# Attention and feed-forward on one core: two batches' head-sum transposes and the last batch's key and query transposes in other units

## The reference, cut to what matters

```python
x = hidden
x = x + global_latent_attn(rmsnorm(x, norm1_w), g_wq, g_kv_down, g_k_up, g_v_up, g_wo)
x = x + local_gqa_attn(rmsnorm(x, norm2_w), l_wq, l_wk, l_wv, l_wo)
...
q, k = (rope(q, BASE_L), rope(k, BASE_L))
q, k = (qk_norm(q), qk_norm(k))
scores = jnp.einsum('bhqd,bhkd->bhqk', q, k) / np.sqrt(HD).astype(np.float32)
probs = jax.nn.softmax(scores, axis=-1)
return jnp.einsum('bhqk,bhkd->bhqd', probs, v)
```

## Time and profile before

| what | us |
|---|---|
| median of 3 runs | 1248.83 |
| lowest and highest of them | 1248.32, 1250.73 |
| the profiled execution's time | 1250.4 |
| its span, first to last instruction | 1248.6 |
| the attention stream in it, first exponential of unit 144 to the last addition to the state | 390.5 to 508.2 |

### The profile page before, as it was taken

One profiled execution on the slowest core, in us unless ns is written; L12 is line 12 of the kernel. 1 busy time (PEld: TensorE's weight loads), 2 busy tenths in 40 slices (PEclk: granted clock), 3 DMA queues, 4 the chain that ended last, 5 costly groups with the idle time before them and its releaser, 6 DMA issues.

```text
span 1248.6 us, 37433 instructions
## 1 busy us (share of the span) xinstructions
PE 1122.8 (90%) x16018; PEld 693.9 (56%) x16018; DVE 969.4 (78%) x1540; ACT 815.5 (65%) x1197; POOL 382.5 (31%) x536
## 2 busy tenths in 40 slices
PE   4488889898889989688999999999999999999985
PEld 3133434344445766455666666666666666666662
DVE  6969694869768688886887788778877887887755
ACT  3498898989878857355655665666566555656641
POOL 1203220201201014665533333343334333433310
PEclk8599999999999989898999999999999999999997
DMA  3113131022113541110211111111111100101102
GB/s 108 34 23 129 47 107 34 19 93 95 34 50 119 169 151 54 51 27 19 75 28 23 28 28 23 28 28 23 28 23 28 27 22 21 34 22 23 28 6 68
DMA packets 41684, 61.71 MB, mean 49 GB/s; under 512 B 7440, under 2 KB 16816, under 8 KB 41520
## 3 DMA queue, kind: packets, MB, share of 16 engines
q1 hardware_dynamic: 39728, 58.44, 16.0%
q10 hardware_dynamic: 1792, 0.87, 0.3%
HBM read 22.61 MB, written 16.78 MB: 32 GB/s over the span
## 4 chain that ended last, share of the span: by engine, by line
PE 52%; DVE 4%; ACT 2%; issue 1%; DVEq 0%; ACTq 0%
PE psum L1374 9%; PE psum L1510 7%; PE psum L1463 6%; PE psum L1485 5%; PE psum L1449 5%; PE psum L1384 4%; PE psum L1394 4%; PE psum L1536 3%; PE psum L1471 2%; PE psum L1434 2%; PE psum L1406 2%; ACT ffn_probs L1693 2%; PE psum L1440 1%; PE psum L1414 1%; PE psum L1502 1%
## 5 line engine op out<-in xcount | busy, mean ns | idle before, releaser
L863 ACT ACTIVATE att_probs<-psum 128x1024 f32<-128x1024 f32 x352 | 335.2, 1027 | 39.0 <-PE psum L721 38.8
L1804 POOL TENSOR_TENSOR ffn_rot<-ffn_rot,ffn_rot_sin 128x512 f32<-128x512 f32 x128 | 160.0, 1271 | 373.4 <-DVE ffn_rot L1835 373.4
L762 PE MATMUL psum<-att_probs,att_v 128*32 128x256 f32 (+3 forms) x3072 | 178.1, 346 | 3.8 <-DVE att_probs L1056 3.2
L721 PE MATMUL psum<-att_q_stack,att_k_parts 64*128 64x512 bf16 (+2 forms) x1472 | 134.4, 276 | 42.0 <-ACT att_probs L863 30.8
L721 PEld LDWEIGHTS psum<-att_q_stack,att_k_parts 64*128 64x128 bf16 x1472 | 45.6, 95 | 141.5 <-ACT att_probs L863 103.6
L1686 ACT ACTIVATE ffn_max_t<-psum 68x128 bf16<-68x128 bf16 x64 | 17.5, 273 | 156.8 <-PE psum L1422 156.6
L762 PEld LDWEIGHTS psum<-att_probs,att_v 128*32 128x32 f32 x3072 | 79.5, 110 | 63.5 <-issue 38.9
L1056 DVE TENSOR_TENSOR att_probs<-att_probs,att_causal_mask 128x1024 f32<-128x1024 f32 (+1 forms) x80 | 94.8, 1201 | 25.7 <-ACT att_probs L863 25.4
L1693 ACT ACTIVATE ffn_probs<-psum 128x1024 f32<-128x1024 f32 x64 | 65.6, 1025 | 59.2 <-PE psum L1449 59.2
L1655 ACT ACTIVATE ffn_sq<-psum 128x512 f32<-128x512 f32 x128 | 74.6, 595 | 21.8 <-PE psum L1374 20.9
L1463 PEld LDWEIGHTS psum<-ffn_v_back,ffn_probs 128*64 128x64 f32 x1024 | 64.5, 137 | 31.8 <-ACT ffn_probs L1693 18.0
(11 more groups left out here) (225 smaller groups left out, 2404.0 us busy)
## 6 DMA issues: line engine op xcount, KB each, us to landing
ffn_v_back<-ffn_v SPq DMA_DIRECT2D x120, 130.0 KB, 2.4
att_q_stack<-q_rows SPq DMA_DIRECT2D x28, 512.0 KB, 3.7
q_rows<-att_q_high SPq DMA_DIRECT2D x21, 256.0 KB, 2.8
q_rows<-att_q_mid SPq DMA_DIRECT2D x21, 256.0 KB, 2.6
q_rows<-att_q_low SPq DMA_DIRECT2D x14, 256.0 KB, 3.6
xres<-in_hidden SPq DMA_DIRECT2D x4, 512.0 KB, 6.2
out<-ffn_qk_t SPq DMA_DIRECT2D x3, 512.0 KB, 3.2
tail_f_wqkv<-in_f_wqkv SPq DMA_DIRECT2D x1, 768.0 KB, 5.5
```

What stands on the lines that cost most here:

```text
L721: ins = T.matmul(psum[:, banks[i] + at:banks[i] + at + width], k_parts[rows, p % 3, j, key:key + P], q_stack[rows, turn % 2, j, q0:q0 + wi ...
L762: ins = T.matmul(psum[32 * g:32 * g + V_PAD, (4 + cc) * BANK + lo - cc * BANK: (4 + cc) * BANK + hi - cc * BANK], v_of(p, kt, g, shift), p ...
L863: act.activation(probs[:, n % E_BUFS, 2 * j:2 * j + 2, 0:width], ps2((step % 2) * 2).rearrange("p (h c) -> p h c", h=2)[:, :, 0:width], AC ...
L1804: steps.did(pool.tensor_tensor(out, out, halves(k.rot_sin[:, n % 2, :])[:, :, 1 - half, :], ALU.add), g["added"] if half else None)
```

## The change

Two tables get other numbers; nothing else is changed, and each engine executes the same instructions.

```diff
-OUT_AT = ((24, 41, 62, 69), (74, 88, 93, 96), (99, 114, 117, 120), (130, 147, 148, 149),
-          (156, 159, 163, 164), (165, 167, 169, 170), (172, 174, 177, 178))
+OUT_AT = ((24, 41, 62, 69), (74, 88, 93, 96), (99, 114, 117, 120), (136, 147, 148, 149),
+          (156, 158, 160, 161), (165, 167, 169, 170), (172, 174, 177, 178))
...
-                  newton=7, rotate=8, k_split=9, q_transpose=10, q_hi=10, q_lo=11, k_transpose=11, k_hi=11, k_lo=12))
+                  newton=7, rotate=8, k_split=11, q_transpose=11, q_hi=11, q_lo=12, k_transpose=13, k_hi=13,
+                   k_lo=14))
```

## The result

| what | before | after |
|---|---|---|
| median, us | 1249.93 (10 runs) | 1256.41 (10 runs) |
| lowest and highest, us | 1248.32, 1251.87 | 1251.96, 1257.62 |
| the profiled execution's time | 1250.4 | 1256.0 |
| its span | 1248.6 | 1254.2 |
| mean granted clock of TensorE in it | 0.966 | 0.959 |

The ratio is **1.0049, 95% interval 1.004 to 1.0059**: the changed kernel is slower by some 6 us, where 1250.7 was forecast. The time lies above the range, which ended at 1253.2.

The account below looks back on a forecast made before the run. Exponentials on ACT were taken to pace the global part and PE the local part. Place one's -2.6 us and place two's +4.5 gave +1.9 us, taking the median from 1248.83 to 1250.7, range 1246.0 to 1253.2.

Parts of the forecast that it names:

- Place one: Tick 130: moving open0 to tick 136 removes ACT's waits around unit 131; -2.6 us, bounds -3.7 and -1.3.
- the price: Tick 136: ACT idles behind open0's eight transposes in their new place; 1.0 us added.
- the change does not remove place one's wait: Rival: unit 131's scores wait for something else; sum about +4 us; no own chance, held within the 30% slower case.
- DVE has no room for open0 at tick 136: Rival: DVE's lag stalls k_transpose of p = 6, then open1 and close; +3.4 us, 1252.2; chance 30%.
- The hole before close: Tick 160: PE's 3.55 us wait before q_transpose becomes some 2.1 us before close, behind open1's arithmetic on DVE.
- The low clock behind it: After the hole before close, PE's rows are slow; without this the chain is 1.5 us shorter.
- The end of q_lo: DVE finishes the last phase's query parts at 460.2 us in place of 455.50.
- place two: Ticks 161 and 162 up to unit 167: DVE's later query parts delay the gather; +4.5 us, bounds +1.1 and +5.
- waits under 1 us: PE's wait before the last phase's k_transpose, 2.10 us before the change, falls under 1 us.
- The way from q_lo to the landing: From q_lo's end to the landed gather of units 166 and 167: 9.8 us of SP issuing and transfer.
- The forecast wait of 5 to 6 us at unit 166: PE, ready at about 464.1 us, waits for the gather landing at 470.0.
- the gather is not the bound: Rival: PE enters unit 166 at 464.1 us without waiting for the gather; -5.2 us, 1243.6; chance 12%.

Follow-up runs that it names:

- e1: Kernel before with only open0 of the fourth phase moved from tick 130 to 136; 1248.01 us, ratio 0.9985.
- e3: Changed kernel, POOL's gated addition of the first batch also waiting for the last block's query split; 1253.26 us, ratio 1.0027 against before.
- e9: Changed kernel, POOL's additions of the first batch waiting for the scores of unit 166, SP's order unchanged; 1253.42 us, ratio 1.0031 against before.
- e4: Changed kernel, SP issuing the gather of units 166 and 167 ahead of the last phase's spread and shifts; 1249.44 us, ratio 1.0001 against before.
- e6: Changed kernel, only the last block's six shifts put behind the gather of units 166 and 167; 1252.54 us, ratio 1.0018 against before.
- e8: Changed kernel, gather of units 166 and 167 issued first and POOL's first-batch additions behind unit 166's scores; 1245.89 us, ratio 0.9972 against before.
- e11: The same kernel as e8, timed again beside e1's kernel; 1246.02 us, ratio 0.9972 against before.

## Why the prediction was wrong, point by point

- **Place one: the mechanism right, the term too large.** The waits went as said, the price was 1.00 us as said, and the trace gives -2.81 where -2.6 was forecast. But the 2.60 us of the earlier trace rows held some 1.1 us of low clock, which not every execution has. The medians give -1.7 to -2.3. The "at the least 2.6" for the gain was read from one execution as if it were the kernel's. The rival "the change does not remove place one's wait" is refuted by the same rows.
- **The rival "DVE has no room for open0 at tick 136": refuted.** e1 is faster than before, and in the trace of the changed kernel the offset of -1.05 us stays constant from unit 137 to 158.
- **The hole before close: right.** 2.33 us, released by L1210, and nothing ahead of q_transpose.
- **The low clock behind it: right in kind, too long.** Close takes 1.94 us, but the rows are back at 0.39 to 0.40 by the second half's scores (445.07), and this gave back some 0.3 us.
- **The end of q_lo: the step that failed.** Forecast 460.2 in the time of before; it ended at 461.90, with the shift of 1.05 us 462.95. The rows were added up at their old lengths (1.2 for the mask, 3.5 for the key split), with the sentence "the additions of p = 4 come earlier, but POOL and the end of the stage hang on p = 5's". That sentence is wrong: POOL's addition of the first batch waits for the addition of p = 4 alone. It started at 449.81, beside the mask (+1.0 us) and the cast (+2.07 us). Less the 0.3 us above that is the 2.75 us by which q_lo came late. e3 takes these away, and the time falls by 3.2 us; e9 takes them away too, and both have a place two near the forecast's +4.5 (+5.3 and +3.9).
- **k_transpose "waits under 1 us": wrong for the same reason.** It waits 3.60 us; in e3 it is 0.64. Behind the longer wait TensorE's granted clock is 0.50 from 460 to 464 us, which the forecast did not have there.
- **The way from q_lo to the landing: right.** 10.4 us in place of 9.8; the low parts' issuing took 2.31 us where the earlier trace rows have 1.05. The forecast wait of 5 to 6 us at unit 166 is 5.71 us, but that its size came right is luck: in the time of before TensorE was ready at 467.7 and not at 464.1, the gather landed at 473.4 and not at 470.0, and the two errors cancel. e4 and e6 show that it is the order of issues that makes the wait.
- **The rival "the gather is not the bound": refuted** by the 5.71 us and by e4.

So place two was +8.1 in the traces for the +4.5 forecast, 2.75 of the 3.6 being q_lo's end and 0.6 the way from there to the landing. Of the 5.7 us between forecast and median, 3.6 are this, about 1 is place one's low clock, and 1.1 is that the median of before is 1249.93 over ten runs where it was 1248.83 over three. The upper bound of the range failed with the same step: +5 for place two took a longer shift into account, but no neighbour on the memory that DVE works in.

The Trainium skill (SBUF — State Buffer, "Who interferes with whom") has the rule that was passed over: a DVE instruction with two inputs in SBUF, or in a mode that uses two ports, and a GpSimd instruction that reads SBUF can't go on together; the later one is blocked until the first has ended. For the mask, which has two inputs in SBUF, the traces agree with it to about a tenth of a microsecond; the cast has one input, and that it ran in a mode with two ports no row shows, only that it was held in the same way. POOL's first part ends at 449.81 + 2.37 = 452.18 and the mask at 453.26, 1.08 us later; POOL's second ends at 455.48 and the cast at 456.10, 0.62 us later. So each ran nearly its whole length after POOL had let go. In e3 the second mask ends at 459.84, 1.07 us behind POOL's 458.77, and the third at 463.14, 1.09 us behind 462.05. The row of the kernel before at 466.18 fits too (468.41, 1.09 us behind POOL's 467.32). Had what waits for the addition of p = 4 been looked up, both late ends could have gone into the sum.

The other sentence of the Trainium skill that the prediction weighed, that the time to initiate a DMA is usually small relative to the DMA (DMA: Bandwidth & Descriptors, "Issuing engines are not separate DMA queues"), speaks of one DMA. For one shift here it is some 0.62 us of issuing with the landing 1.9 to 2.8 us after the issue began. But six of them stand ahead of the gather, 4.0 us in all against the 3.9 of the gather itself, and the sum decides: e6 moved the six and won 4 us.

## What to carry to other kernels

When a step is moved to an earlier place, list everything that waits for it, on the idle engines too, and write down where that work will now run and beside which instructions of the pacing chain; an engine that sat on a semaphore for 70 us is the first to look at. When a chain is late through a DMA, read the issuing queue's order before the arithmetic: putting one DMA ahead of the eight and six that stood before it was worth 7 us here, mending the arithmetic ahead of it alone 3. And let a second execution say how long a wait is before it is booked as a gain.

## What the runs showed of the hardware

- **One hole, two clocks.** Behind TensorE holes of the same length the granted clock fell in one execution and stayed full in another. At place one it is 0.61 and 1.00 behind 2.30 us (above). At place two it is e8 and e11, the same kernel, behind a hole of 2.33 and 2.32 us before close; windows of e8, then of e11:

```profile
441.50:443.50 2.00, 2.00 (x59) 1.80 (x59) 2.00 (x3) 2.00 (x4) 0.00 (x0) 1.00 0.24 34
```

```profile
441.50:443.50 2.00, 2.00 (x39) 1.39 (x37) 2.00 (x3) 2.00 (x3) 0.00 (x0) 0.50 0.00 0
```

  The exponentials of unit 162 start at 445.43 in e8 and at 447.10 in e11. Such a coin was worth 1.5 us at place one and 1.4 at place two, and the executions of one kernel differ by 2 to 8 us in all. What decides it was not tried.

- **POOL is held up as well.** Its multiplication takes 2.37 us when it comes first (after the change, 449.81) and 3.20 us when a mask is already running (e3, 455.57 behind 455.34).
- **Issue times on SP vary.** The last block's two low parts took 1.05 us of SP before, 2.31 after, 2.28 in e6. The six shifts took 0.61 to 0.64 us each, but for single longer ones (1.24 before, 1.69 in e11).
